# Cross-attention decoder layer on one core: two products per tile for weights times V, f16 maxima, a reordered first turn

## The reference

```python
x = _layernorm(x + self_attention(x))      # 16 heads of 16, 4 key groups
# cross-attention: 8 heads of 128, batch folded into the sequence
q, k, v = heads(x @ Wq), heads(ctx @ Wk), heads(ctx @ Wv)   # [8, 1792, 128], [8, 6000, 128] x2
sim = q @ k.T * 128 ** -0.5
mean = jnp.mean(sim, axis=-1, keepdims=True)
sim = (sim - mean) * 1.5 + mean
out = softmax(sim) @ v                      # each query attends to all 6000 keys
x = _layernorm(x + merge(out) @ Wout + bout)
x = _layernorm(x + ffn(x))                  # ternary W1, W2, gelu
```

## Time and profile before

| | |
|---|---|
| times shown (3 runs) | 2537.59, 2559.56, 2567.26 us; median 2559.56 |
| profiled execution | 2544.14 us, span of its instructions 2542.1 us |
| busy share of the span | PE 94%, DVE 82%, ACT 75%, POOL 72% |
| mean granted TensorE clock | 0.978 of full speed |
| DMA | 41.75 MB, mean 16 GB/s |

### The profile page before, as it was taken

One profiled execution on the slowest core, in us unless ns is written; L12 is line 12 of the kernel. 1 busy time (PEld: TensorE's weight loads), 2 busy tenths in 40 slices (PEclk: granted clock), 3 DMA queues, 4 the chain that ended last, 5 costly groups with the idle time before them and its releaser, 6 DMA issues. The chain is left out here.

```text
span 2542.1 us, 69034 instructions
## 1 busy us (share of the span) xinstructions
PE 2401.3 (94%) x28954; PEld 2159.6 (85%) x28954; DVE 2090.2 (82%) x2308; ACT 1896.2 (75%) x2215; POOL 1830.2 (72%) x1090
## 2 busy tenths in 40 slices
PE   6998899999999999999999999999999999999587
PEld 4785799899989998999888988999899989998575
DVE  6565788888888888888887888888888888888877
ACT  4333688888887888788887888788788888888334
POOL 7301399778987898788877897798778877899401
PEclk9797999999999999999999999999999999999899
DMA  6100000000000000000000000000000000012111
GB/s 176 45 0 24 7 6 4 6 6 4 6 6 4 6 6 6 4 6 6 4 6 5 6 6 6 4 6 6 3 7 6 6 4 6 4 57 50 54 53 29
DMA packets 31180, 41.75 MB, mean 16 GB/s; under 512 B 2000, under 2 KB 26032, under 8 KB 30896
## 3 DMA queue, kind: packets, MB, share of 16 engines
q1 hardware_dynamic: 30896, 37.63, 5.2%
HBM read 26.55 MB, written 11.07 MB: 15 GB/s over the span
## 5 line engine op out<-in xcount | busy, mean ns | idle before, releaser
L1047 POOL TENSOR_TENSOR e_lo<-ring,e_hi 128x1024 f16<-128x1024 f32 (+1 forms) x672 | 1403.1, 2101 | 170.0 <-ACT ring L836 141.2
L911 DVE TENSOR_TENSOR run_max<-psum,run_max 128x1024 f32<-128x1024 f32 (+1 forms) x616 | 739.5, 1201 | 301.3 <-ACT ring L821 300.5
L682 PE MATMUL psum<-v_all,e_hi 128*128 128x129 f16 (+1 forms) x5264 | 937.4, 219 | 15.7 <-POOL e_lo L1047 15.6
L684 PE MATMUL psum<-v_all,e_hi 128*128 128x128 f16 (+1 forms) x5264 | 938.1, 221 | 0.0
L686 PE MATMUL psum<-v_all,e_lo 128*128 128x129 f16 (+1 forms) x5264 | 935.4, 218 | 0.0
L821 ACT ACTIVATE ring<-psum 128x1024 f32<-128x1024 f32 (+1 forms) x672 | 674.2, 1003 | 271.1 <-PE psum L665 241.1
L929 DVE SCALAR_TENSOR_TENSOR ring<-ring,psum 128x1024 f32<-128x1024 f32 (+1 forms) x672 | 795.8, 1189 | 0.7 <-PE psum L759 0.7
L665 PE MATMUL psum<-qx_hi,k_hi 128*128 128x256 f16 x2632 | 719.5, 273 | 9.3 <-DVE run_max L911 4.6
L665 PE MATMUL psum<-qx_lo,k_hi 128*128 128x256 f16 x2632 | 719.3, 273 | 0.0
L665 PE MATMUL psum<-qx_hi,k_lo 128*128 128x256 f16 x2632 | 719.3, 273 | 0.0
L836 ACT ACTIVATE ring<-ring 128x1024 f32<-128x1024 f32 (+1 forms) x672 | 694.4, 1034 | 4.9 <-DVE ring L929 4.2
(11 more groups left out here) (177 smaller groups left out, 2755.3 us busy)
## 6 DMA issues: line engine op xcount, KB each, us to landing
o_scratch<-o_buf SPq DMA_DIRECT2D x56, 129.0 KB, 2.7
raw<-o_scratch SPq DMA_DIRECT2D x16, 451.5 KB, 3.7
stage<-in_ctxT SPq DMA_DIRECT2D x6, 500.0 KB, 4.0
stage<-in_ctxT SPq DMA_DIRECT2D x12, 250.0 KB, 4.8
scratch<-in_xT SPq DMA_DIRECT2D x1, 1792.0 KB, 7.4
res<-in_x SPq DMA_DIRECT2D x1, 1792.0 KB, 16.9
o_scratch<-res SPq DMA_DIRECT2D x1, 1792.0 KB, 8.1
res<-o_scratch SPq DMA_DIRECT2D x1, 1792.0 KB, 9.6
```

The source lines that it names most:

```text
L682: pe.matmul(out_t, lhsT=e_hi_f[keys, cols], rhs=v_all[keys, tile, 0:OW], start=first, stop=False)
L684: pe.matmul(out_t[:, 0:DH], lhsT=e_hi_f[keys, cols], rhs=v_all[keys, tile, OW:VW], start=False, stop=False)
L911: ins = v.tensor_tensor(run_max[:, 0:n], pair(f)[:, 0:n], run_max[:, 0:n], ALU.max)
L1047: g.tensor_tensor(e_lo[f % NEL][:, 0:n], slot, e_hi[f % NEH][:, 0:n], ALU.subtract).then_inc(s_lo, 1)
```

## The change

1. The two products with the weights' high part become one of 257 columns. As 257 columns for two query halves don't fit one bank, each half has its own bank (4 and 5), for every block; the rest's sum stands in columns 129 to 256 and is added at the exit.
2. Therefore a block's accumulators are not doubled any more. The exit is an ACT copy of the 129 columns (now first thing in turn 0), then `add_low` on VectorE (in turn 0 behind the subtraction), which adds the other 128 columns; the store waits for that. TensorE leaves out `attend` in turn 0 and does turn 0's and turn 1's in turn 1, after waiting for `add_low`. In turn 1 ACT keeps the scores ahead of `exp_half`.
3. The running maximum, its folds and the row maxima are f16; the fold is two element-wise maxima (1024 to 512 to 256) in place of one reduction. Transposes and spread use an f16 identity and an f16 view of bank 7.
4. `spread` stands behind the side task and `attend` in turn 8.

```diff
-        FOLD = RUN + 4096
-        SMALL = FOLD + 1024
+        FOLD = RUN + 2048
+        SMALL = FOLD + 1536
...
+                g.wait_ge(s_const, 1)
+                run(g.tensor_copy(ident16[:, :], ident[:, :]))
...
-        run_max = at(RUN, "run_max", [P, GT * QB], F32)
+        run_max = at(RUN, "run_max", [P, GT * QB], F16)
-        fold = at(FOLD, "fold", [P, QB], F32)
-        row_max = at(SMALL, "row_max", [P, QT], F32)
+        fold2 = at(FOLD, "fold2", [P, 2 * QB], F16)
+        fold = at(FOLD + 1024, "fold", [P, QB], F16)
+        row_max = at(SMALL, "row_max", [P, QT], F16)
...
+        side16 = psum[:, 7, 0:QB // 2].bitcast(F16)
...
-                def attend(f, more, par):
+                def attend(f, more):
...
-                            out_t = psum[:, 4 + par, t * OW:(t + 1) * OW]
-                            first = s == 0 and i == 0 and t == 0
-                            last = last_tile and t == QT - 1
-                            pe.matmul(out_t, lhsT=e_hi_f[keys, cols], rhs=v_all[keys, tile, 0:OW],
-                                      start=first, stop=False)
-                            pe.matmul(out_t[:, 0:DH], lhsT=e_hi_f[keys, cols], rhs=v_all[keys, tile, OW:VW],
-                                      start=False, stop=False)
-                            mm = pe.matmul(out_t, lhsT=e_lo_f[keys, cols], rhs=v_all[keys, tile, 0:OW],
-                                           start=False, stop=last)
+                            pe.matmul(psum[:, 4 + t, 0:VW], lhsT=e_hi_f[keys, cols], rhs=v_all[keys, tile, :],
+                                      start=(s == 0 and i == 0), stop=False)
+                            mm = pe.matmul(psum[:, 4 + t, 0:OW], lhsT=e_lo_f[keys, cols],
+                                           rhs=v_all[keys, tile, 0:OW], start=False, stop=last_tile)
...
-                        mm = pe.transpose(psum[:, 7, t * P:(t + 1) * P], fold[:, t * P:(t + 1) * P], ident[:, :])
+                        mm = pe.transpose(side16[:, t * P:(t + 1) * P], fold[:, t * P:(t + 1) * P], ident16[:, :])
...
-                                       lhsT=row_max[:, t:t + 1].broadcast_to([P, P]), rhs=ident[:, :],
+                                       lhsT=row_max[:, t:t + 1].broadcast_to([P, P]), rhs=ident16[:, :],
...
-                    if s == MAX_S + 2 and -1 <= n < NBLK - 1:
-                        spread(n, n_at, number - 1)
                     task = side_of(n, s)
                     if task is not None and task[0] != "t":
                         side(n, s, past, number)
-                    if n >= 0:
-                        if s == 0 and n >= 2:
-                            pe.wait_ge(s_oev, n_at - 1)
-                        attend(n * NGRP + s, past * NQB * NGRP, n % 2)
+
+                    if n >= 0 and s == 1:
+                        if n >= 1:
+                            pe.wait_ge(s_oev, n_at)
+                        attend(n * NGRP, past * NQB * NGRP)
+                    if n >= 0 and s > 0:
+                        attend(n * NGRP + s, past * NQB * NGRP)
+                    if s == MAX_S + 2 and -1 <= n < NBLK - 1:
+                        spread(n, n_at, number - 1)
...
-                    a.activation(o_buf[:, :, :], psum[:, 4 + n % 2, 0:QT * OW].rearrange(
-                        "p (t w) -> p t w", t=QT), ACT.Copy).then_inc(s_oev, 1)
+                    a.activation(o_buf[:, :, :], psum[:, 4:6, 0:OW], ACT.Copy).then_inc(s_ohi, 1)
...
+                    if s == 0 and n > 0:
+                        store_output(n - 1)
+                    if s == 1 and f + LEAD < NF_ALL:
+                        keep_scores(f + LEAD)
                     if weights % 2 == 0 and 0 <= weights < NF_ALL:
                         exp_half(weights)
-                    if f + LEAD < NF_ALL:
+                    if s != 1 and f + LEAD < NF_ALL:
                         keep_scores(f + LEAD)
...
-                    if s == 1 and n > 0:
-                        store_output(n - 1)
...
-                    v.tensor_reduce(fold[:, :], run_max[:, :].rearrange("p (i q) -> p q i", i=GT), AX.X,
-                                    ALU.max).then_inc(s_fold, 1)
+                    v.tensor_tensor(fold2[:, :], run_max[:, 0:2 * QB], run_max[:, 2 * QB:4 * QB],
+                                    ALU.max).then_inc(s_fold2, 1)
+                    v.wait_ge(s_fold2, n + 1)
+                    v.tensor_tensor(fold[:, :], fold2[:, 0:QB], fold2[:, QB:2 * QB], ALU.max).then_inc(s_fold, 1)
...
+                def add_low(n):
+                    v.wait_ge(s_ohi, n + 1)
+                    v.tensor_tensor(o_buf[:, :, 0:DH], psum[:, 4:6, OW:VW], o_buf[:, :, 0:DH],
+                                    ALU.add).then_inc(s_oev, 1)
...
+                    if s == 0 and n > 0:
+                        add_low(n - 1)
                     if f + LEAD < NF_ALL:
                         running_max(f + LEAD)
...
+                add_low(NBLK - 1)
```

More of the change, by code:

```diff
@@ L80, in build @@
         psum = top.enter_context(nc.psum_tensor("psum", [P, 8, 512], F32))
-        CTX = 15456
+        CTX = 15712
         WQ = CTX + 3 * NKP * 2
@@ L100, in build @@
         ident = at(14336, "ident", [P, P], F32)
-        stats = at(14848, "stats", [T, NB, 6], F32)
-        meanvar = at(15232, "meanvar", [T, NB, 2], F32)
-        rstd = at(15360, "rstd", [T, NB], F32)
-        b1s = at(15424, "b1s", [P, FF // P], F32)
+        ident16 = at(14848, "ident16", [P, P], F16)
+        stats = at(15104, "stats", [T, NB, 6], F32)
+        meanvar = at(15488, "meanvar", [T, NB, 2], F32)
+        rstd = at(15616, "rstd", [T, NB], F32)
+        b1s = at(15680, "b1s", [P, FF // P], F32)
         ctx_hi, ctx_lo, ctx_s = [at(CTX + i * NKP * 2, n, [P, NKP], F16)
@@ L577, in build @@
         o_buf = at(SMALL + 160, "o_buf", [P, QT, OW], F32)
-        (s_qk, s_kept, s_max, s_sub, s_hi, s_exp, s_cast, s_lo, s_av, s_fold, s_bc, s_oev, s_od, s_init) = [
-            sem("b_" + n) for n in ("qk", "kept", "max", "sub", "hi", "exp", "cast", "lo", "av", "fold", "bc",
-                                    "oev", "od", "init")]
+        (s_qk, s_kept, s_max, s_sub, s_hi, s_exp, s_cast, s_lo, s_av, s_fold2, s_fold, s_bc, s_ohi, s_oev, s_od,
+         s_init) = [
+            sem("b_" + n) for n in ("qk", "kept", "max", "sub", "hi", "exp", "cast", "lo", "av", "fold2", "fold",
+                                    "bc", "ohi", "oev", "od", "init")]
         s_side, s_half, s_free = sem("b_side"), sem("b_half"), sem("b_free")
@@ L915, in fold_max @@
                     v.wait_ge(s_max, n * NGRP + NGRP)
-                    v.tensor_reduce(fold[:, :], run_max[:, :].rearrange("p (i q) -> p q i", i=GT), AX.X,
-                                    ALU.max).then_inc(s_fold, 1)
+                    v.tensor_tensor(fold2[:, :], run_max[:, 0:2 * QB], run_max[:, 2 * QB:4 * QB],
+                                    ALU.max).then_inc(s_fold2, 1)
+                    v.wait_ge(s_fold2, n + 1)
+                    v.tensor_tensor(fold[:, :], fold2[:, 0:QB], fold2[:, QB:2 * QB], ALU.max).then_inc(s_fold, 1)
                 def rows_max(number):
                     v.wait_ge(s_side, number + 1)
-                    v.tensor_reduce(row_max[:, :], psum[:, 7, 0:QB].rearrange("p (t k) -> p t k", t=QT), AX.X,
+                    v.tensor_reduce(row_max[:, :], side16.rearrange("p (t k) -> p t k", t=QT), AX.X,
                                     ALU.max).then_inc(s_free, 1)
```

## The result

| | before | after |
|---|---|---|
| median (20 runs of each) | 2546.11 us (2536.29 to 2567.26) | 2561.75 us (2549.34 to 2580.39) |
| ratio to before | | 1.0059, 95% interval 1.0037 to 1.008 |
| span of the profiled execution | 2542.1 us | 2561.2 us |

The change makes the kernel 0.6% slower. The median of 2559.56 shown ahead was that of three runs; twenty give 2546.

A forecast was written before the change was run, and what follows sets the result against it. TensorE's stream was taken to set the period, with a loop over the other engines nearly as long. Block terms of -0.55 us a head made -4 in all: 2544.1 to 2540, plus 10 gives 2550, range 2480 to 2600.

The forecast's parts named there:

- What TensorE sheds: TensorE's products, transposes, spread and waits: 2.3 us less in five blocks of a head, 1.1 in the other two.
- (b): Rival: all that TensorE sheds comes out of the time, 2434, with 10 us added 2444; chance 0.14 including milder cases.
- (d): Rival: a 257-column product costing 0.115 leaves no gain in products, +9 us in all; its chance is inside the forecast's 0.42.
- The loop: Plain block, GpSimd's turn 3 cast through ACT, VectorE and TensorE to the next: 34.25 us, 34.75 with GpSimd held.
- link 2: ACT's copy of scores in turn 8 waits for the ring slot that GpSimd's e_lo of turn 9 frees: +0.1 us.
- A: The start of GpSimd's turn 3 cast in a plain block, from which the forecast counts its times in us.
- two a block: Sign that the forecast is right: the wait of ACT's copy for e_lo grows to two in each block.
- The hold-up of GpSimd: Two fold operations with two SBUF inputs hold GpSimd 0.5 us in a plain block, bounds 0.3 and 0.7.
- Rival (a): The fold doesn't hold GpSimd, plain blocks stay as now: 2516 us, with 10 us added 2526; chance 0.24.
- Rival (c): Second fold operation also loses to turn 9's e_lo, ending at 19.6: +52 us, 2592, with 10 added 2602; chance 0.20.
- The other blocks: Blocks with k or v tasks: first -0.85 us, fifth -0.2, the two with sides in nearly all turns -0.5 each.
- the 10 us added for the spread of the runs shown: Whole kernel: 10 us put on the summed 2540, as the profiled run lay low among those shown, giving 2550.

The follow-up runs named there:

- the swap in ACT's queue: Changed kernel with ACT's copy of turn 9's scores moved ahead of the exponential half: 2538.86 us, ratio 0.9976.
- the maxima alone: Only parts 3 and 4 of the change, with three products, doubled accumulators and the old exit: 2523.0 us, ratio 0.9913 to before.
- the first experiment: Changed kernel with its fold as one reduction again, everything else as changed: 2576.41 us, ratio 1.0101 to before.

## Why the prediction was right and where it was wrong

- **What TensorE sheds.** A pair of products takes 0.168 (939.17 to 939.34) against the 0.172 of three: 0.4 us a block, forecast 0.5. Transposes to scores 0.13 (923.94 to 924.07), forecast 0.11; the wait at the spread gone. Right, and worth nothing as forecast: rivals (b) and (d) fall.
- **The loop.** Right link by link, 34.38 against 34.75, and confirmed by the swap in ACT's queue (-0.7), by the early spread (turn 8 longer, turn 0 shorter, same block) and by the maxima alone (33.5). One reading in link 2 was off and did no harm: turn 8's scores were to be there at A + 18.0, but the forecast's own A + 17.8 for the end of the fold puts their end at A + 19.3. Their last start is 925.27, A + 18.83, half a us ahead of the copy's slot, and with the slower reduction they are what the copy waits for. The sign "two a block" for ACT's waits on `e_lo` was too low as well: the plain block has five.
- **The hold-up of GpSimd.** There, but 0.2 instead of 0.5: the second operation ran into the cast, as forecast, and nothing else was held. The plain block is so 0.14 longer than before, not 0.5. Rival (a) wanted 34.25, and the run without the hold gave 34.37, since the slower reduction took its place. Rival (c) did not come: the second operation ended at 923.89, 17.45 behind turn 3's cast, near the 17.8 of the forecast.
- **The step that failed: "The other blocks".** It had -0.85, -0.2, -0.5 and -0.5 for the first, fifth, sixth and seventh block; measured are -0.32, +1.2, +0.38 and +0.83. The forecast's sign hung on it: the plain blocks alone were to be 1.5 longer a head (measured 0.4). For the first the level was right (34.75; 34.74), but the 35.60 taken for it before was the stretch between two output copies, and from turn 2 to turn 2 it was 35.06. For the last three it priced the side bank only at turn 9, and put its wait at turns 0 and 1 at nothing. There is one, bank 7: a side product waits until ACT has read the former one for the high half and VectorE for the low half. Before, turn 0's products stood between the side products of turn 0 and turn 1; the change takes them away, and only one set of scores is left. TensorE and VectorE at turns 0 and 1 of the sixth block:

```profile
1011.03 0.38 PE L698 MATMUL psum<-ctx_s,wk_s_lo 128*128 128x512 f16 x1
1011.25 0.27 PE L673 MATMUL psum<-qx_hi,k_hi 128*128 128x256 f16 x1
...
1013.31 0.39 PE L698 MATMUL psum<-ctx_hi,wk_hi 128*128 128x512 f16 x1 [0.58 <-DVE k_lo L906]
```
```profile
1011.43 1.23 DVE L918 TENSOR_TENSOR run_max<-psum,run_max 128x1024 f16<-128x1024 f32 x1
1012.57 0.68 DVE L906 SCALAR_TENSOR_TENSOR k_lo<-psum,k_hi 128x512 f16<-128x512 f32 x1
```

  The scores take 1.3 us; the way of the side product through ACT and VectorE, 2.3 from its last start to 1013.31. Turns 0 and 1 together grow from 7.53 to 8.21 in the sixth block (+0.7, in the stretch of the fifth) and from 7.60 to 8.25 in the first block of the next head (in that of the seventh). Turns 0 and 1 of the seventh block add 0.2. The run with turn 0's products back in turn 0 takes the 0.6 to 0.7 of the sixth and of the first block away again (7.60 in both).
- **The late spread and the same bank.** The maxima's part, the late spread above all, makes the larger part of the loss in these blocks: alone it adds 1.09, 0.28 and 0.28 to them, and the spread put back early takes 0.77, 0.46 and 0.49 off. At turn 9 of each the loss is 0.75, where the forecast had 0.75 for the fifth and 0.55 for the others; with the spread early 0.5 to 0.8 of it go, and with the low half ahead of the subtraction all of it, with the old exit (3.77, 3.50, 3.80) and with the new one (3.73, 3.46, 3.77). In the fifth block, besides, the gain of the late spread doesn't arrive: turn 8's side product uses the same bank as the transposes and waits for the row maxima (L698 behind L930, 0.8), so turn 8 gives 0.27, where it gives 1.29 in the plain blocks and the forecast had 1.25. That is 1.0 more than forecast, the largest term of the fifth block's miss.
- **Turn 3** of the sixth and seventh block grows by 0.2 and 0.1. Its side product starts 0.2 after its scores, as the low half of turn 2's ends only then; that stands behind the running maximum and a copy of ACT's that waited for GpSimd:

```profile
1019.38 1.02 ACT L827 ACTIVATE ring<-psum 128x1024 f32<-128x1024 f32 x1 [0.90 <-POOL e_lo L1065]
...
1021.58 0.68 DVE L906 SCALAR_TENSOR_TENSOR k_lo<-psum,k_hi 128x512 f16<-128x512 f32 x1
...
1022.32 0.39 PE L698 MATMUL psum<-ctx_hi,wk_hi 128*128 128x512 f16 x1
```

  It goes with turn 0's products back in turn 0 (3.73), and not with ACT's high half of turn 1 ahead (3.94). Why GpSimd is late there was not tested.

Together, for the fifth block, the largest single miss: +0.68 (turns 0 and 1), +0.30 (turn 7), -0.27 (turn 8), +0.75 (turn 9) and -0.25 over the rest are the +1.2. The forecast had for the same places 0, +0.75, -1.25, +0.75 and -0.5. That block alone makes 8.7 of the 19 us.

That the time came so near the forecast is in part luck. The plain blocks were forecast 1.1 us a head too long, which covers a quarter of the 4.1 by which the others were forecast too short; and the 10 us added for the spread of the runs shown were not there: the median of twenty is 2 us above the profiled execution.

## What to carry to other kernels

When products are moved in TensorE's stream, look at every bank that is used in turn around them: work between two uses of a single buffer is its cover, and whoever takes it away pays the buffer's way through the other engines. Write the exit of a block as a loop over all engines before giving up a second set of accumulators; here 0.4 us of TensorE's work a block was bought for 36 to 39 us of the kernel, in all three settings in which it was measured. And try the order of two neighbours in an in-order queue first: two such swaps, with no change in the work, took 37 us off the kernel with the maxima alone.

## What the hardware showed that was not expected

- TensorE's clock after a wait. After a wait of 2.60 us in the kernel with turn 0's products in turn 0, the granted clock stays at 1.00 during the wait, falls after it, and stands at 0.50 (1.2 in place of 2.4 GHz) from 946.60 to 949.40; score products are then 0.21 apart instead of 0.11. It doesn't follow every time: from 300 to 2200 us 23 of the 28 waits of 2.60 to 2.67 us in that kernel have such a fall behind them, one of 2.44 and the seven of 1.52 have none; in after the one wait of 2.27 (at 1363) has one and that of 1.35 has none. The plain block shown has 34.02 of busy TensorE, for the same products that take 32.52 in after, so the 2.6 of wait cost more than 2.6.

```profile
945.24 0.28 PE L687 MATMUL psum<-v_all,e_hi 128*128 128x257 f16 x1 [2.60 <-DVE o_buf L942]
...
946.93 0.42 PE L673 MATMUL psum<-qx_hi,k_hi 128*128 128x256 f16 x1
947.15 0.42 PE L673 MATMUL psum<-qx_lo,k_hi 128*128 128x256 f16 x1
```

- TensorE's clock ahead of the blocks. From 60 to 240 us, in the self-attention, the granted clock averages 0.88 in the profiled execution with the earliest first scores (241.0 us, turn 0's products in turn 0), 0.82 in before and after (252) and 0.73 in the one with the latest (272.2, spread early); in the twelve executions profiled the first scores never start earlier at a lower clock. From 300 to 2200 us it is 1.00 in all but the first of these (0.98). Why it differs between executions isn't shown.

- VectorE beside GpSimd. The price of an operation with two SBUF inputs is not fixed: the first fold (922.39, 0.45) began as GpSimd's pair at 918.33 was ending; the second, beside the cast at 922.50, took 1.01 for half the columns, and the cast lost 0.2. The Trainium skill (SBUF — State Buffer, section Who interferes with whom) has such a pair contend and a reduction not; the trace agrees, with 1.24 against 1.04 for the same cast, and 1.04 again beside the reduction of the first experiment.
